# Attention stage: the tail term added at the eviction of a head's values, and scores as three products of rounded parts

## The reference, cut to what matters

```python
gate = q_flat @ Wg
delta = v_flat @ Wd
bias = (jax.nn.sigmoid(gate) * delta).transpose(0, 2, 1)
scores = jnp.einsum('bngqd,bnkd->bngqk', q, k) * scale
logits = scores + bias[:, :, None, None, :]
allowed = causal[None, None, None] & (bias > 0)[:, :, None, None, :]
neg = jnp.finfo(logits.dtype).min
logits = jnp.where(allowed, logits, neg)
p = jax.nn.softmax(logits, axis=-1)
o = jnp.einsum('bngqk,bnkd->bngqd', p, v)
```

## Time and profile before

| | |
|---|---|
| runs | 5260.47, 5268.34, 5271.86 us |
| profiled execution, its own time | 5256.53 us |
| its span, first to last instruction | 5254.7 us |
| TensorE, PE | 4563.9 us busy, 87% |
| its weight loads, PEld | 3716.7 us, 71% |
| VectorE, DVE | 2863.7 us, 54% |
| ScalarE, ACT | 2072.3 us, 39% |
| GpSimd, POOL | 1425.4 us, 27% |
| first and last scores pass of the attention stage | 3548.2 and 5004.7 us |

### The profile page before, as it was taken

The page is one execution under the profiler, slowest core; times in us unless marked ns, Lnnn a source line. Parts: engine busy times, 40 slices in busy tenths (PEclk is TensorE's granted clock), DMA queues, the critical chain, the costliest instruction groups (busy, mean ns, idle before and its releaser), DMA issues. The chain is left out here.

```text
span 5254.7 us, 87865 instructions
## 1 busy us (share of the span) xinstructions
PE 4563.9 (87%) x27638; PEld 3716.7 (71%) x27638; DVE 2863.7 (54%) x7411; ACT 2072.3 (39%) x5463; POOL 1425.4 (27%) x2882
## 2 busy tenths in 40 slices
PE   3588888988898888888888868978999999999979
PEld 3477777777777777777777757865666666666668
DVE  5555555555555555555555533425555555555545
ACT  2244444444444444444444412214444444444422
POOL 4233333333333333333333315620000000000024
PEclk9999999999999999999999979979999999999989
DMA  7332333222223332322333222221111111111011
GB/s 275 95 91 82 93 93 93 84 88 80 88 84 92 93 92 85 92 88 84 93 93 93 84 77 85 72 68 41 42 44 44 40 31 44 40 44 40 22 53 33
DMA packets 568788, 401.09 MB, mean 76 GB/s; under 512 B 261488, under 2 KB 513392, under 8 KB 566896
## 3 DMA queue, kind: packets, MB, share of 16 engines
q1 hardware_dynamic: 568304, 395.08, 24.4%
HBM read 296.75 MB, written 98.14 MB: 75 GB/s over the span
## 5 line engine op out<-in xcount | busy, mean ns | idle before, releaser
L886 DVE SCALAR_TENSOR_TENSOR g_conv<-g_r,g_taps,g_conv 128x511 f32<-128x511 f32 (+2 forms) x960 | 713.7, 743 | 136.6 <-ACT g_conv L785 119.8
L789 ACT ACTIVATE g_us<-g_chn 128x128 f32<-128x128 f32 x528 | 146.2, 277 | 952.6 <-PE g_chn L612 951.8
L590 PE MATMUL g_lev<-g_nu,g_T 128*128 128x128 f32 (+1 forms) x3120 | 437.3, 280 | 20.1 <-DVE g_nu L898 20.1
L559 PE MATMUL g_r<-g_x_hi,g_w_hi 128*128 128x512 f32 x768 | 356.0, 464 | 101.3 <-issue 68.2
L2195 POOL TENSOR_TENSOR a_bias<-a_kb,a_start 128x128 f32<-128x128 f32 (+2 forms) x96 | 56.6, 618 | 1381.8 <-DVE a_low L2064 941.6
L917 DVE SCALAR_TENSOR_TENSOR g_S<-g_S,g_ctab,g_chn 128x128 f32<-128x128 f32 x396 | 137.6, 347 | 526.6 <-PE g_chn L622 526.6
L583 PE MATMUL g_lev<-g_U,g_L 128*128 128x128 f32 x2340 | 346.5, 285 | 84.9 <-DVE g_L L925 43.2
L590 PEld LDWEIGHTS g_lev<-g_nu,g_T 128*128 128x128 f32 (+1 forms) x3120 | 372.9, 177 | 59.3 <-DVE g_nu L898 32.3
L1922 ACT ACTIVATE a_pr<-a_pr,a_low 128x128 f32<-128x128 f32 (+3 forms) x512 | 286.9, 560 | 314.4 <-DVE a_low L2064 310.5
L1712 PE MATMUL a_sc<-a_kT,a_qT 128*128 128x128 f32 (+3 forms) x1024 | 341.1, 460 | 60.9 <-DVE a_low L2064 56.9
L1061 POOL TENSOR_TENSOR g_prod<-g_small 64x14 f32<-64x14 f32 (+6 forms) x896 | 227.1, 254 | 587.1 <-DMA g_small<-lower_d 521.9
(11 more groups left out here) (347 smaller groups left out, 11386.9 us busy)
## 6 DMA issues: line engine op xcount, KB each, us to landing
g_w_hi<-ws_d SPq DMA_DIRECT2D x65, 768.0 KB, 5.4
g_w_lo<-ws_d SPq DMA_DIRECT2D x65, 768.0 KB, 6.5
lower_d<-g_L SPq DMA_DIRECT2D x64, 512.0 KB, 3.2
g_T<-low_d SPq DMA_DIRECT2D x64, 512.0 KB, 4.1
g_U<-upp_d SPq DMA_DIRECT2D x64, 512.0 KB, 5.3
a_w<-w_groups SPq DMA_DIRECT2D x32, 640.0 KB, 4.6
oT_d<-g_oT SPq DMA_DIRECT2D x67, 256.0 KB, 5.3
f_oT<-oT_d SPq DMA_DIRECT2D x8, 2048.0 KB, 9.0
```

The lines of the kernel that those rows point to most:

```text
L559: mm = M.matmul(BANK[n][:], a[:, k, n, :], c[:, k, :], start=(i == 0), stop=(i == len(terms) - 1))
L590: mm = M.matmul(lev[hf][0:rows, c, :].rearrange("p (j n) -> p j n", j=2), T[0:rows, hf * HC + c, 0:rows], nu[0:rows, hf * HC + c, :].unsqu ...
L886: ins = V.scalar_tensor_tensor(out=y[:, k:L], in0=x[:, 0:L - k], scalar=tap, in1=y[:, k:L], op0=ALU.mult, op1=ALU.add)
```

## The change

**Tail term.** `tail_rows` now leaves the sum of later values transposed, as 12 columns of `pb` (128 x 4 x 3), by 12 fp32 matmuls whose stationary operand is a value tile and whose moving operand has 3 columns. VectorE copies them to `vtT`. The flags go another way round: VectorE writes them to `fl` (128 x 3), GpSimd multiplies them with the identity to `dg` (128 x 384, rounded), TensorE multiplies that by ones in one pass, so that each partition of `pb` holds all flags. VectorE multiplies by `vtT` to `tl` (128 x 384), once per turn. The two three-row matmuls per head are gone. `head_out` moves from ScalarE (a copy) to VectorE (`out` + `tl`).

**Scores.** q and k are each kept as `hi` (written by ScalarE from `pa`) and `lo` (`pa` - `hi`, by VectorE after it). The scores of a tile are `product` of them, three rounded passes in place of one fp32 matmul. VectorE's copy of q becomes the subtraction and now waits for ScalarE, whose new copy stands behind the exponentials of the head before. The key's copy by ScalarE is followed by a subtraction on VectorE that did not exist.

```diff
             def tail_rows(bp):
-                for m in range(1, TT):
-                    mm = M.matmul(pb[0:TAIL, :], cc["tails"][:, m * TAIL:(m + 1) * TAIL], v[bp][:, m, :], start=(m == 1), stop=(m == TT - 1))
+                for n in range(HKV):
+                    for m in range(1, TT):
+                        mm = M.matmul(pb[:, TAIL * P + n * TAIL:TAIL * P + (n + 1) * TAIL], v[bp][:, m, n * P:(n + 1) * P],
+                                      cc["tails"][:, m * TAIL:(m + 1) * TAIL], start=(m == 1), stop=(m == TT - 1))
                 mm.then_inc(s["vtp"], 1)
...
-                    M.matmul(sc[i % 2][:, 0:width(i)], qT[g % 2][:, i * P:(i + 1) * P], kT[tp_][:, 0:width(i)], start=True, stop=True).then_inc(s["sc"], 1)
+                    at = slice(i * P, (i + 1) * P)
+                    product(sc[i % 2][:, 0:width(i)], [(q_hi[g % 2][:, at], q_lo[g % 2][:, at], k_hi[tp_][:, 0:width(i)], k_lo[tp_][:, 0:width(i)])]).then_inc(s["sc"], 1)
...
             def flag_rows(t):
-                pe.wait_ge(s["fl"], t + 1)
-                for i in range(TAIL):
-                    mm = M.transpose(pb[0:TAIL, i * P:(i + 1) * P], fl[:, i, :], ident)
-                mm.then_inc(s["ftr"], 1)
+                pe.wait_ge(s["dg"], t + 1)
+                M.matmul(pb[:, 0:TAIL * P], ones[:], dg[:].rearrange("p i n -> p (i n)"), start=True, stop=True).then_inc(s["ftr"], 1)
...
-                if g == 0:
-                    pe.wait_ge(s["frow"], t + 1)
-                M.matmul(out[:, 0:TAIL * P], vt_hi[:, at], frow[:], start=False, stop=False)
-                M.matmul(out[:, 0:TAIL * P], vt_lo[:, at], frow[:], start=False, stop=True).then_inc(s["pv"], 1)
+                mm.then_inc(s["pv"], 1)
...
-                if n == 0 or more:
+                if n and more:
                     pe.wait_ge(s["frow"], t + 1)
...
                 exps(t, 1)
+                query(t, 2)
                 evac(t, 0)
-                if not begin:
-                    head_out(t - 1, there, 3)
-                if n == 0:
-                    tail_rows(b)
...
             def query(t, g):
-                dve.wait_ge(s["q"], G * t + g + 1)
-                V.tensor_copy(qT[g % 2][:], pa[:]).then_inc(s["qT"], 1)
+                dve.wait_ge(s["q_hi"], G * t + g + 1)
+                V.tensor_tensor(q_lo[g % 2][:], pa[:], q_hi[g % 2][:], ALU.subtract).then_inc(s["qT"], 1)
+
+            def key(t, tp_):
+                dve.wait_ge(s["k_hi"], t + 1)
+                V.tensor_tensor(k_lo[tp_][:], pa[:], k_hi[tp_][:], ALU.subtract).then_inc(s["kT"], 1)
...
-            def flag_rows(t):
+            def flag_rows(t, b, n, tp_):
+
                 dve.wait_ge(s["ftr"], t + 1)
-                V.tensor_copy(frow[:], pb[0:TAIL, 0:TAIL * P]).then_inc(s["frow"], 1)
+                dve.wait_ge(s["vtT"], b + 1)
+                V.tensor_tensor(tl[tp_][:, 0:TAIL * P].rearrange("p (i l) -> p i l", i=TAIL), pb[:, 0:TAIL * P].rearrange("p (i l) -> p i l", i=TAIL),
+                                vtT[:, n, :].unsqueeze(2).to_broadcast([P, TAIL, P]), ALU.mult).then_inc(s["frow"], 1)
+
+            def head_out(t, tp_, g):
+
+                dve.wait_ge(s["pv"], G * t + g + 1)
+                dve.wait_ge(s["frow"], t + 1)
+                V.tensor_tensor(oT[tp_][:, g, :], out[:], tl[tp_][:], ALU.add).then_inc(s["oT"], 1)
...
+            def diagonals(t):
+
+                pool.wait_ge(s["fl"], t + 1)
+                if not (isinstance(t, int) and t == 0):
+                    pool.wait_ge(s["ftr"], t)
+                Gp.tensor_tensor(dg[:], cc["ident"].unsqueeze(1).to_broadcast([P, TAIL, P]), fl[:].unsqueeze(2).to_broadcast([P, TAIL, P]),
+                                 ALU.mult).then_inc(s["dg"], 1)
```

More of the change, by code:

```diff
@@ L1548, in attention @@
         bias = two("bias", [P, TT, L])
-        kT, v = two("kT", [P, L]), two("v", [P, TT, NK * P])
-        vt_hi, vt_lo = (sb(f"vt_{i}", [TAIL, NK * P], F32R) for i in ("hi", "lo"))
-        qT, pr = two("qT", [P, L]), two("pr", [P, TT, L])
+        k_hi, k_lo, v = two("k_hi", [P, L], F32R), two("k_lo", [P, L], F32R), two("v", [P, TT, NK * P])
+        q_hi, q_lo, pr = two("q_hi", [P, L], F32R), two("q_lo", [P, L], F32R), two("pr", [P, TT, L])
+        vtT, tl = sb("vtT", [P, HKV, TAIL]), two("tl", [P, L])
+        fl, dg = sb("fl", [P, TAIL]), sb("dg", [P, TAIL, P], F32R)
+        one, ones = sb("one", [P, P]), sb("ones", [P, P], F32R)
         low, tot = two("low", [P, TT]), two("tot", [P, TT])
         cnt, rec = sb("cnt", [P, TT]), sb("rec", [P, TT])
-        fl, frow = sb("fl", [P, TAIL, TAIL]), sb("frow", [TAIL, TAIL * P], F32R)
         pt = two("pt", [P, L * TT - P * 6])
@@ L1848, in turn @@
                     value_rows(1 - bp, 1)
+            pe.wait_ge(s["one"], 1)
             pe.wait_ge(s["in"], 16 * 6)
@@ L1916, in key, with query @@
                 act.wait_ge(s["k"], t + 1)
-                A(kT[tp_][:], pa[:], ACT.Copy).then_inc(s["kT"], 1)
+                A(k_hi[tp_][:], pa[:], ACT.Copy).then_inc(s["k_hi"], 1)
+            def query(t, g):
+                act.wait_ge(s["q"], G * t + g + 1)
+                A(q_hi[g % 2][:], pa[:], ACT.Copy).then_inc(s["q_hi"], 1)
             def exps(t, g):
@@ L1938, in turn @@
                 exps(t, 1)
+                query(t, 2)
                 evac(t, 0)
-                if not begin:
-                    head_out(t - 1, there, 3)
-                if n == 0:
-                    tail_rows(b)
-                elif n == 1 and more:
+                if n == 1 and more:
                     columns(b + 1, 1 - bp, 0, pb)
@@ L1952, in turn @@
                 exps(t, 2)
+                query(t, 3)
                 evac(t, 1)
-                head_out(t, here, 0)
                 if n == 0 and more:
@@ L1957, in turn @@
                 exps(t, 3)
+                if nxt:
+                    query(t + 1, 0)
                 evac(t, 2)
-                head_out(t, here, 1)
                 if more or n < 2:
@@ L1965, in turn @@
                     exps(t + 1, 0)
+                    query(t + 1, 1)
                 evac(t, 3)
-                head_out(t, here, 2)
                 if n == 1 and more:
@@ L1982, in _ @@
             key(0, 0)
+            query(0, 0)
             for m in range(TT):
                 value_rows(0, 0, m)
+            query(0, 1)
             exps(0, 0)
             loop(act, turn)
-            head_out(LAST, 1, 3)
         @block.vector
@@ L2104, in turn @@
                 normalise(t, 1)
-                flag_rows(t)
+                if not begin:
+                    head_out(t - 1, there, 3)
                 if n == 0:
                     tail_rows(b)
-                elif n == 1 and more:
+                flag_rows(t, b, n, here)
+                if n == 1 and more:
                     columns(b + 1, 1 - bp, 0, pb)
@@ L2113, in turn @@
                     diagonal(t + 1, there, (n + 1) % HKV, nb, kb_count(b, bp, n))
+                    key(t + 1, there)
                 logits(t, 2, here)
@@ L2153, in _ @@
             dve.wait_ge(s["init"], 1)
+            V.tensor_copy(ones[:], one[:]).then_inc(s["one"], 1)
             stats_of(0)
@@ L2171, in _ @@
             gate_end(0)
+            key(0, 0)
             query(0, 0)
@@ L2179, in _ @@
             loop(dve, turn)
+            head_out(LAST, 1, 3)
             add_out(LAST, 1, 0)
@@ L2186, in _ @@
             Gp.memset(eps[:], LN_EPS)
-            Gp.memset(fl[:], 0.0)
+            for t in tl:
+                Gp.memset(t[:], 0.0)
+            Gp.memset(one[:], 1.0)
             Gp.memset(start[:], 0.0).then_inc(s["init"], 1)
```

27 lines of the change are left out of this document (13 added, 14 removed).

## The result

Four runs of the changed kernel took 5211.27 to 5223.87 us, median 5215.86; four of the kernel before, on the same chip, 5260.47 to 5273.67, median 5270.1. The ratio is 0.990, 95% interval [0.988, 0.992]: faster by 54 us. The forecast was 5237, a gain of 31; the measured time lies in the forecast's range, 5207 to 5284, near its lower end. The profiled executions differ by less: 5215.72 against 5256.53, 41 us. The stretch from the first scores pass of the attention stage to the first pass of the last head's scores holds the gain. It was 1454.1 us (3548.2 to 5002.4) and is 1404.4 (3559.7 to 4964.2), 49.7 less. The delta-rule stage, which the change does not touch, ended at 3125.8 before and 3136.7 after (start of its last TensorE pass), 10.9 later. Over all profiles of this study it ended between 3125.8 and 3142.8.

What follows compares the result with a forecast made beforehand. TensorE was taken to bound the attention stage, with VectorE late next in sections A and D. Per batch -6.1 us, times 8 = -49, +2 stage start, +16 clock = -31: 5268 - 31 = 5237 us, range over all 5207 to 5284.

Steps and rivals of the forecast that it cites:

- The chain of VectorE: From one head's scores' end: subtraction done at 3.15 us, normalise 5.54, eviction 6.2, next tile 2 starts 6.5, scores end 7.7.
- the prices of passes: TensorE passes: 0.112 us for 128 or 256 rounded columns, 0.17 for 384, 0.232 for 512; three passes a tile, 1.9 us.
- B: Head-to-head section with output projection, eviction and split hidden: saves 0.55 (tail) + 0.39 (scores) = 0.94 us; four give -3.76.
- C: Another section with output projection, same savings, 0.39 or 0.29 for scores: on average 0.89 us; four give -3.56 a batch.
- A, n = 0: Section without projection, in the batch's n = 0 turn, with all 24 tiny passes: 12.98 to 12.07 us, -0.9, before clock falls.
- section A with its clock: Section without projection where TensorE awaits flags: +2.7 and -0.9 us a batch, plus clock falls +12.5 (n = 0), +3.5 (n = 2).
- n = 1 to 3: Other turns' flags sections: TensorE restarts 0.2 us later, split key delays scores 0.65; about +0.9 each, +2.7 a batch.
- The stage's start: Start of the attention stage: first key and query are split in a chain, adding about 2 us once.
- Section D: Section without projection, VectorE becomes late: 7.67 to 7.7 us, no gain; +0.25 after n = 1, -0.80 after n = 2; -0.55 a batch.
- Rival 1: Slower: the clock falls in most sections A, 24 sections at 2.5 to 3.4 us each, 5281 to 5303 us; chance 0.15.
- Rival 2: No change: VectorE's chain waits 0.7 us more in the 64 sections A and D, about 5263 us; chance 0.13.
- rival 3: Larger gain: exponentials end earlier, no clock falls, D saves 0.4 us each too, -60, 5208 us; chance 0.06.

Runs made afterwards that it cites:

- e_flags: Changed kernel with VectorE's flags multiply ahead of the eviction of the last turn's fourth head, for n = 1 to 3; 5207.9 us, ratio 0.988.
- e_per_turn: Changed kernel, but each turn makes only its own group's three tail columns, six passes in place of 24 at n = 0; 5200.7 us, ratio 0.987.
- e_scores: Kernel before with only the scores' three rounded products and split q and k, old tail term kept; 5280.4 us, ratio 1.002.
- e_norm: Changed kernel with VectorE's normalise ahead of the subtraction of q and the copy of `pt`; 5210.9 us, ratio 0.990.
- e_tail: Changed kernel with fp32 scores and plain copies of q and k, so only the new tail term; 5190.5 us, ratio 0.986.

## Why the prediction was right, and where it was off

**The chain of VectorE and the prices of passes** held to 0.2 us, as shown above. In the scores of section A at 4072 passes of 128 columns start 0.11 us apart, of 384 0.17 to 0.18. B fell by 3.66 us a batch (forecast 3.76), C by 3.32 (3.56). A, n = 0 without a fall of the clock took 12.03 in e_flags (12.07).

**The term mis-sized** is section A with its clock, by some 18 us. Forecast for n = 1 to 3 was +2.7, and +3.5 / 8 for the clock of n = 2, together +3.1 a batch. Measured: +0.57, -0.21 and +0.80, together +1.2; eight times the difference is 16. Nearly all of it is n = 2. The fall there did not grow. Before, it lasted 6.8 us in six of the seven batches that have gate passes, and 3.4 in one; after, 3.4 us in four, 6.8 in two and 10.2 in one. Nor does it cost as much where it is as long: with 6.8 us the section took 16.0 to 16.1 us before and 15.6 to 15.7 after. Take the batch of the earlier trace rows. Before, the fall began at 4212.35, on the gate passes, and all of its 6.83 us lay on passes of TensorE. After, it begins at 4206.2, when those passes are over. It slows the key's last passes and then scores that wait for VectorE's split key anyway. From the restart behind the flags to the end of the next scores it took 9.59 us before (4210.27 to 4219.86) and 8.97 after (4202.70 to 4211.67), the wait for the split key among them. So the slow clock and that wait, which I added, partly cover each other. For n = 0 I had -0.9 and five falls of 2.5, +0.66 a batch. Measured is +0.40: the clock fell in all eight batches, but at the price of 1.3 us that e_per_turn took out. That the two are so near is luck: the count was too low and the price too high, and the count itself is one of this profile.

**The stage's start** was counted at 2 us; from the end of the delta rule to the first scores it took 422.4 us before and 423.0 after.

**Section D** came out at -0.9 a batch, forecast -0.55. That this is nearly what B and C together lack (0.34) is luck again. After n = 1 I had +0.25 for the split of rows, and it is -0.9 (9.17 to 8.26): TensorE had that section's transposes in addition and was the bound up to the scores, so its saving counts, while its wait inside the scores stayed (0.97 and 1.00 us in one batch). Two costs that I had not seen offset this. One is the clock: in D, n = 1 (+0.36) it fell in five of eight batches, behind a wait inside the scores, which TensorE's timeline shows:

```profile
4321.64 0.44 PE L1669 MATMUL a_sc<-a_k_hi,a_q_hi 128*128 128x384 f32 x1 [1.71 <-DVE a_low L2061]
...
4322.70 0.63 PE L1669 MATMUL a_sc<-a_k_hi,a_q_lo 128*128 128x512 f32 x1
```

VectorE's split of a weight tile stands ahead of those logits. The other is the back edge.

**The back edge.** At turns 12 and 20, where the loop over two batches begins again, TensorE stands still with nothing that the profile shows to wait for. Before, and after, in D of turn 12:

```profile
4111.23 2.65 PE L1712 MATMUL a_sc<-a_kT,a_qT 128*128 128x128 f32 x8 [1.35 <-issue]
```

```profile
4106.21 0.32 PE L1669 MATMUL a_sc<-a_k_hi,a_q_hi 128*128 128x128 f32 x1 [2.54 <-issue]
```

D, n = 0 was 9.1 to 9.2 us there and 7.8 elsewhere; after, 11.1 to 11.3 against 7.7; in e_scores, 13.6 against 7.6. So a back edge costs 1.4 us before, 3.5 after and 6 in e_scores. The stall itself is 1.35, 2.5 to 2.9, and in e_scores 2.1 and 2.4 one after the other; the rest is a fall of the clock on the scores behind it. In sum it costs the changed kernel 4 us more than the kernel before, and e_scores 9. Why it is this long is not shown by any run.

**What GpSimd did** I had priced at nothing, since the flags' product hides. It does, but I did not follow the queue to the instruction behind it. For the changed kernel itself the price was right: the multiplies of its sections D kept their 1.28 us, and of the small instructions one takes 0.27 for 0.15. As soon as the order on VectorE moved (e_norm) or its chain got shorter (e_tail), the spreading fell on them; in e_norm taking it away gave 16 us.

**The rivals.** Rival 1 had the place wrong: in no A with n = 1 or 3 did the clock fall, though TensorE idles 1.5 us there, and behind the tiny passes it fell every time in this profile. The rule of the Trainium skill that the prediction weighed (TensorE: Matmul & The Clock Gate, section "HAM oscillation — how this bites in real kernels"), idle gaps between bursts, would have `tail_rows` cost nothing; the granted clock of 0.51 behind them does not bear it out. Rival 2's longer chain did not come, and rival 3's 5208 was nearer the truth than its chance of 0.06 said, for other reasons: the clock did fall, and D saved 0.9 a batch where that rival needs 2.2.

**The range.** The forecast's own range of 5212 to 5257 does not follow from its terms, which give 5268 - 47 - 5 = 5216 to 5268 - 47 + 35 + 5 = 5261. The measured 5216 is at the lower end of both. S gained 50 us where the terms gave 31; section A with its clock is 18 of the difference, and D's surplus and the shortfall of B and C cancel. No run tells what the other 4 us of the medians' 54 are.

## What to carry to other kernels

When a change puts a new instruction into a third engine's queue, follow what stands behind it: its cost may be where that one now runs. Two losses on the same stretch, a slow clock and a wait, must not be added. And split a change with two ideas early: here one half brought 76 us and the other took 22 back.

## What the runs showed of the hardware

- Passes of 3 or 8 columns cost as much as 256 rounded columns (0.112 us) and more by what follows: in the changed kernel the clock fell to its 1.2 GHz level behind every run of 24, over all kernels that keep the 24 passes of three columns in 32 of 56 batches. Behind six it never did (32 batches): the falls of e_per_turn that touch A, n = 0 began ahead of its six. In the changed kernel a fall made that section 1.1 to 1.8 us longer.
- Beside GpSimd's additions on SBUF tiles VectorE's addition of two SBUF tiles took 0.32 us (e_norm) and 0.75 (e_tail) for 0.16, and four multiplies 1.96 for 1.27; readers of a bank were not touched (0.68 and 0.69).
- The untouched delta-rule stage varied by 17 us between profiles of kernels that differ only after it, more than several of the effects studied. Runs of one kernel differ by 13 us (e_tail, mean granted clock 0.973 and 0.969) to 20 (e_flags, 0.970 and 0.965).
